# A fused attention and expert kernel on one core: packs, rows of maxima, score banks and the order of projections around its first two attentions

## Reference

```python
x = x + L0_xattn(_layernorm(x), ctx)     # self-attention, cross-attention, FFN (1024), a norm behind each
x = x + L0_ffn(_layernorm(x))            # one 256x256 linear layer plus a low-rank part
x = x + L1_xattn(_layernorm(x), ctx)     # masked cross-attention, 77 keys
x = x + L1_ffn(_layernorm(x))            # gated single-head attention and 8 experts
```

```python
sa = _mha(x, x, x, Wq1, Wk1, Wv1, bv1, causal=True)      # 16 heads of 16, 1024 x 1024 scores
x  = layernorm(sa + x, g1, be1)
ca = _mha(x, ctx, ctx, Wq2, Wk2, Wv2, bv2, causal=False) # 77 keys
x  = layernorm(x + ca, g2, be2)
x  = layernorm(x + relu(x @ Wf1 + bf1) @ Wf2 + bf2, g3, be3)
```

## Time and profile before

| | us |
|---|---|
| median of 3 runs (1371.41 to 1375.86) | 1371.98 |
| the profiled execution | 1369.3 |
| its span in the trace | 1367.3 |

### The profile page before, as it was taken

The page is one execution under the profiler, slowest core; times in us unless marked ns, Lnnn a source line. Parts: engine busy times, 40 slices in busy tenths (PEclk is TensorE's granted clock), DMA queues, the critical chain, the costliest instruction groups (busy, mean ns, idle before and its releaser), DMA issues. The chain is left out here.

```text
span 1367.3 us, 19836 instructions
## 1 busy us (share of the span) xinstructions
PE 1201.6 (88%) x7072; PEld 844.6 (62%) x7072; DVE 856.5 (63%) x1816; ACT 565.2 (41%) x1202; POOL 315.6 (23%) x490
## 2 busy tenths in 40 slices
PE   7888888888888798999888786899989888899999
PEld 3443333323333336677667665899977777688998
DVE  4487666677656666666568786766644355955555
ACT  5215566656565553455225542210013233543332
POOL 5011222222121036444127651000010111500000
PEclk8999999999998767999889987999999989999999
DMA  5850373330444601000011000000030000000000
GB/s 198 166 131 1 55 62 47 48 48 1 70 72 71 122 4 56 1 1 1 1 74 50 2 0 1 1 1 1 0 123 1 0 1 1 1 1 17 16 17 16
DMA packets 37968, 50.69 MB, mean 37 GB/s; under 512 B 11098, under 2 KB 28784, under 8 KB 37232
## 3 DMA queue, kind: packets, MB, share of 16 engines
q1 hardware_dynamic: 37872, 49.44, 17.3%
HBM read 37.26 MB, written 11.77 MB: 36 GB/s over the span
## 5 line engine op out<-in xcount | busy, mean ns | idle before, releaser
L545 PE MATMUL PS<-ARENA 128*17 128x512 f32 (+17 forms) x2208 | 410.1, 430 | 71.2 <-DVE ARENA L1708 23.9
L545 PEld LDWEIGHTS PS<-ARENA 128*17 128x17 f32 (+6 forms) x2208 | 164.5, 127 | 249.7 <-issue 109.9
L1322 ACT ACTIVATE ARENA<-PS 128x512 f32<-128x512 f32 (+3 forms) x384 | 177.0, 491 | 140.8 <-PE PS L545 134.6
L1708 DVE TENSOR_REDUCE ARENA<-PS 128x1 f32<-128x128 f32 (+7 forms) x256 | 179.7, 750 | 74.1 <-PE PS L545 73.3
L545 PE MATMUL PS<-WQKVP,TRR 128*128 128x384 f32 x512 | 133.0, 341 | 3.1 <-DVE ARENA L2012 2.0
L2174 POOL TENSOR_SCALAR_AFFINE_SELECT ARENA<-ARENA 128x128 f32<-128x128 f32 x256 | 74.9, 299 | 202.5 <-ACT ARENA L1322 198.6
L2142 POOL TENSOR_TENSOR rstd<-var,halves 128x4 f32<-128x4 f32 x36 | 38.4, 1065 | 281.9 <-DVE var L1553 232.7
L545 PEld LDWEIGHTS PS<-W2P,INT 128*128 128x128 f32 x768 | 95.1, 188 | 2.9
L545 PE MATMUL PS<-W2P,INT 128*128 128x256 f32 x768 | 95.5, 280 | 0.0
L545 PEld LDWEIGHTS PS<-WQKVP,TRR 128*128 128x128 f32 x512 | 92.6, 190 | 4.1 <-DVE ARENA L2012 2.3
L545 PE MATMUL PS<-TRR,W1P 128*128 128x512 f32 x256 | 88.4, 406 | 7.1 <-ACT BC L1248 7.1
(11 more groups left out here) (228 smaller groups left out, 1971.9 us busy)
## 6 DMA issues: line engine op xcount, KB each, us to landing
ARENA<-qk_parts SPq DMA_DIRECT2D x96, 128.0 KB, 5.7
...
ARENA<-in_w SPq DMA_DIRECT2D x2, 2048.0 KB, 10.8
...
```

The costliest lines, as they stand in the source:

```text
L545: return nc.tensor.matmul(o, lhsT, rhs, start=start, stop=stop, **kw)
L1322: ins = nc.scalar.activation(PROB[GRP * (step % 2) + j][:, 0:w], PS[:, uses[key][0], 0:w], ACT.Exp, scale=HD ** -0.5)
L1708: ins = v.tensor_reduce(negm[:, n % 2, TPB * j + st:TPB * j + st + 1], PS[:, bank:bank + 2, :].rearrange("p b s -> p (b s)")[:, 0:P * (st ...
```

## The change

It has five parts.

- **Start.** The projections of a batch run chunk by chunk (`projection`), so that the first needs only its first chunk's transposes. SP stores the 64 rows of group 0 first and loads its query half and key half each as soon as that half's store has landed; `load_pack(1)` comes after all stores of batch 0. Fillers before the first maximum: 8 for 36.
- **Third score bank.** Self-attention's scores use banks 4, 5 and 7; both halves of the values share bank 6, and every group's output is copied and turned in two halves (`evach`, `outh`), the first in the middle of its own block.
- **Chunk order.** The second chunk's queries are made in block 7 instead of 8, and SP stores them before group 7's rows of maxima. In block 8 the maxima of chunks 0 and 1 come one per unit, and norm, turn and queries of chunk 2 some units earlier.
- **Third chunk's packs.** `XPACK[2]` lies in ranges of its own (part of `SA` and `VEXT` that batch 0 used), so SP loads it without waiting for the last scores; `XPROB` moves and the cross stage's output goes to `XO`. Rows of chunks 2 and 3 are issued by POOL, behind `xneg` in its order. Some slots move up by one to three, and `xpv` of eight steps (`FILLED_STEPS`) gets 2 fillers.
- **Last norm.** Pieces 1 to 5 of the fourth chunk's second norm come after DVE's split of the FFN's second weight, and POOL's power for it after its first eight lower parts.

```diff
             if u == 1 and n > 1:
-                yield "evac", n - 2
+                yield "evach", n - 2, 1
             if u == OUT_AT and n > 1:
-                yield "out", n - 2
+                yield "outh", n - 2, 1
+            if u == 19 and n > 0:
+                yield "evach", n - 1, 0
+            if u == 23 and n > 0:
+                yield "outh", n - 1, 0
...
                 yield from context_plan(u - 6)
-            if n in (7, 8):
-                c, at = n - 7, u - (8, 2)[n - 7]
-                if at in (0, 2):
-                    yield "xq", c, at // 2
-                if at in (4, 6):
-                    yield "xqm", c, at // 2 - 2
+            if n == GROUPS - 1:
+                for c, first in enumerate((8, 26)):
+                    at = u - first
+                    if at in (0, 2):
+                        yield "xq", c, at // 2
+                    if at in (4, 6):
+                        yield "xqm", c, at // 2 - 2
             if n == GROUPS:
-                if u == 20:
-                    yield "evach", n - 1, 0
+                if u < 8:
+                    yield "xmax", 0, u % 4, u // 4
+                if u == 9:
+                    yield "xneg", 0
+                if 14 <= u < 22:
+                    yield "xmax", 1, (u - 14) % 4, (u - 14) // 4
                 if u == 23:
-                    yield "outh", n - 1, 0
-                if u >= 25 and u % 2 == 1 and u < 25 + 2 * NORM_PIECES:
-                    yield "norm", 2, u // 2 - 12
-                if u == 43:
+                    yield "xneg", 1
+                if 24 <= u < 24 + NORM_PIECES:
+                    yield "norm", 2, u - 24
+                if u == 37:
                     yield "turn", 2
-                if u in (45, 47):
-                    yield "xq", 2, u // 2 - 22
-            if n == GROUPS and u % 2 == 0:
-                if 6 <= u < 22:
-                    yield "xmax", 0, (u - 6) // 2 % 4, (u - 6) // 8
-                if u == 22:
-                    yield "xneg", 0
-                if u >= 32:
-                    yield "xmax", 1, (u - 32) // 2 % 4, (u - 32) // 8
+                if u in (39, 41):
+                    yield "xq", 2, u // 2 - 19
+                if u in (44, 46):
+                    yield "xqm", 2, u // 2 - 22
...
     yield "evach", GROUPS - 1, 1
-    yield "xneg", 1
...
+def projection(step):
+    g, at = divmod(step, 4)
+    return g, at % 2, at // 2
...
     yield from out(XSTEPS - 1)
+FILLED_STEPS = (0, 5, 6, 7, 11, 12, 13, 14)
...
     put(0, 0, "outh", GROUPS - 1, 1)
-    for g in range(2):
-        put(0, 1 + g, "xqm", 2, g)
     for piece in range(NORM_PIECES):
-        put((piece + 3) // 4, (piece + 3) % 4, "norm", 3, piece)
-    put(3, 0, "turn", 3)
-    put(3, 2, "xq", 3, 0)
+        put((piece + 1) // 4, (piece + 1) % 4, "norm", 3, piece)
+    put(2, 3, "turn", 3)
+    put(3, 1, "xq", 3, 0)
...
     put(4, 2, "xqm", 3, 1)
-    for m, (t, j) in enumerate(((3, 1), (3, 2), (4, 0), (4, 3), (5, 0), (5, 1), (5, 2), (5, 3))):
+    for m, (t, j) in enumerate(((2, 1), (3, 0), (3, 2), (4, 0), (4, 3), (5, 0), (5, 1), (5, 2))):
         put(t, j, "xmax", 2, m % 4, m // 4)
-    put(6, 0, "xneg", 2)
-    for piece, (t, j) in enumerate(((6, 2), (6, 3), (7, 0), (7, 1), (7, 2))):
+    put(5, 3, "xneg", 2)
+    for piece, (t, j) in enumerate(((6, 0), (6, 1), (6, 2), (6, 3), (7, 0))):
...
         XPACK = [[region(lo, 2048).bitcast(BF16).rearrange("p (h s) -> p h s", h=HH) for lo in pair]
-                 for pair in ((4096, 10240), (0, 6144), (2048, 8192), (4096, 10240))]
+                 for pair in ((4096, 10240), (0, 6144), (14336, 22528), (4096, 10240))]
...
         KPARTS = region(30736, 462).bitcast(BF16).rearrange("p (g c t) -> p g c t", g=2, c=3)
-        XPROB = [region(22528 + 512 * s, 512, parts=T) for s in range(8)]
+        XPROB = [region(lo + 512 * j, 512, parts=T) for lo in (8192, 24704) for j in range(GRP)]
+        XO = region(2048, 2048, "p (i f) -> p i f", i=2 * GRP)
...
             return c if rest == 0 and 0 <= c < 4 else None
+        def load_rows(eng, c):
+            eng.wait_ge(xmparts_ready, c + 1)
+            for g in range(2):
+                for r in range(3):
+                    eng.dma_start(XPACK[c][g][ROWS + r:ROWS + r + 1, :, :].rearrange("o h (t s) -> o (h t) s", s=P),
+                                 xmparts[32 * g:32 * g + 32, c % 2, r, :]).then_inc(xrows_in[c], 16)
...
                 banks = ((2, 3, 4, 5, 6, 7), (6, 7, 4, 5))[b]
-                if step == 0:
-                    for c in (2 * b, 2 * b + 1):
-                        turn("t_in", "in", H, c, ((0, 1), (4, 5))[b], 14 if c == 0 else 0)
-                    for c in (2 * b, 2 * b + 1):
-                        turned("t_in", c)
+                if step < 2:
+                    turn("t_in", "in", H, 2 * b + step, ((0, 1), (4, 5))[b], 14 if (b, step) == (0, 0) else 0)
+                if step in (0, 2):
+                    turned("t_in", 2 * b + step // 2)
                 if step < 8:
-                    g, w, c = step // 4, step // 2 % 2, step % 2
+                    g, w, c = projection(step)
...
                             claim("idle", [0], 0, 0)
-                            busy(36, 0)
+                            busy(8, 0)
...
                     w = 512 * c + 512 - lo
-                    bank = 4 + narrow
+                    bank = (4, 5, 7)[ring % 3]
...
                     filled(ins, ("score", n, tt, c, j))
-                    narrow = 1 - narrow
+                    ring += 1
...
                     if (tt, c) == (0, 0):
-                        if n < GROUPS - 1:
-                            claim(("values", n), [6, 7], signals=0)
-                        else:
-                            for half in range(2):
-                                claim(("values", n, half), [6 + half], signals=0)
+                        claim(("values", n, 0), [6], signals=0)
...
                             drained(pe, ("v1", i))
+                    if (tt, c) == (0, 1):
+                        claim(("values", n, 1), [6], signals=0)
...
                     for j in range(GRP):
-                        ins = mm(PS[32 * j:32 * j + VW, 6 + c, lo - 512 * c:512],
+                        ins = mm(PS[32 * j:32 * j + VW, 6, lo - 512 * c:512],
...
                     claim(("xv", n), [bank])
+                    busy(2 if n in FILLED_STEPS else 0, bank)
...
                      a[name].rearrange("(o e) -> o e", o=1).broadcast_to([P, EXPERTS]))
+            def load_half_pack(n, w):
+                b, h0 = n // 4, GRP * (n % 4)
+                packs, order = ((PACKQ, QPART), (PACKK, KPART))[w]
+                src = scratch[b, w].rearrange("(h e) c s -> c e h s", h=HEADS)
+                for r, part in enumerate(order):
+                    sp.dma_start(packs[n % SLOTS][HD * r:HD * r + HD, :, :],
+                                 src[part, :, h0:h0 + GRP, :]).then_inc(pack_in[n % SLOTS], 16)
             def load_pack(n):
-                b, h0 = n // 4, GRP * (n % 4)
-                for w, packs, order in ((0, PACKQ, QPART), (1, PACKK, KPART)):
-                    src = scratch[b, w].rearrange("(h e) c s -> c e h s", h=HEADS)
-                    for r, part in enumerate(order):
-                        sp.dma_start(packs[n % SLOTS][HD * r:HD * r + HD, :, :],
-                                     src[part, :, h0:h0 + GRP, :]).then_inc(pack_in[n % SLOTS], 16)
-            for u in range(8):
-                b, g, w = u // 4, u // 2 % 2, u % 2
-                sp.wait_ge(parts_ready, 2 * (u + 1))
-                sp.dma_start(scratch[b, w, P * g:P * g + P, :, :], PARTS[u % 4]).then_inc(parts_out[u], 16)
-                if u == 1:
-                    for v in (0, 1):
-                        sp.wait_ge(parts_out[v], 16)
-                    load_pack(0)
-                    load_pack(1)
+                for w in range(2):
+                    load_half_pack(n, w)
+            def store_parts(b, g, w, lo=0, hi=P):
+                sp.wait_ge(parts_ready, 8 * b + 4 * g + w + 3)
+                sp.dma_start(scratch[b, w, P * g + lo:P * g + hi, :, :], PARTS[2 * g + w][lo:hi]).then_inc(parts_out[4 * b + 2 * g + w], 16)
+            for w in range(2):
+                store_parts(0, 0, w, 0, GRP * HD)
+            for w in range(2):
+                sp.wait_ge(parts_out[w], 16)
+                load_half_pack(0, w)
+            for w in range(2):
+                store_parts(0, 0, w, GRP * HD, P)
+            for w in range(2):
+                store_parts(0, 1, w)
+            for w in range(2):
+                sp.wait_ge(parts_out[w], 32)
+            load_pack(1)
+            for u in range(4):
+                store_parts(1, u // 2, u % 2)
...
                     load_pack(n + 2)
-            send_queries(1)
...
             load_queries(1)
-            load_rows(0)
-            load_rows(1)
+            load_rows(sp, 0)
+            load_rows(sp, 1)
```

(37 more changed lines are left out.)

92 lines of the change are left out of this document (37 added, 55 removed).

## The result

The changed kernel takes 1355.07 us (median of 4 runs, 1352.71 to 1356.99) against 1371.70 (4 runs, 1371.14 to 1375.86) of the kernel before: a ratio of 0.9872, 95% interval 0.9846 to 0.9897. Timed again beside other kernels it was 1352.49 against 1367.66, 0.989 (0.9848 to 0.9932). So the change gains 15 to 17 us, about half of the 32.8 of the forecast. 1355 lies inside the range given (1323 to 1361), but not in the 1328 to 1350 to which the forecast gave 0.45.

A forecast was written before the change was run, and what follows sets the result against it. TensorE's (PE's) order of work, its waits and its clock were taken to bound the kernel; 7 + 1 + 6 + 2 + 14 + 2.8 = 32.8 us gained, giving 1339 us (forecast 1328 to 1350, range 1323 to 1361).

The forecast's parts named there:

- block 8: Self-attention's block 8: score waits go and chunk 0's row maxima come one per score; 2 us gained, bounds -2 and 4.
- (a): Cross stage keeps its low clock because light work, not waits, lowers it; no gain there, total 1353 us; chance 0.20.
- (c): Cross stage: POOL issues DMAs at 2 us each, each chunk's rows come 6.6 us later; total 1352 us; chance 0.10.
- Start: Before the first maximum: chunk-first projections and half packs bring it from 51 to 44 us; 7 gained, bounds 4 and 9.
- (e): Start: half packs fail because stores keep the DMA engines full; gain 0 to 2 us, total 1345 us; chance 0.08.
- Block 0: Self-attention's first block, 51 to 101 us: PE idles less though its clock still falls; 1 us gained, bounds -1 and 3.
- Third score bank: Blocks 1 to 7: scores stop waiting for exponentials in block tails, up to 0.89 us each; 6 us gained, bounds 0 and 10.
- the mark set for a wrong prediction: Self-attention: the prediction counts as wrong if blocks 1 to 7 together are not 3 us shorter.
- Cross stage: Cross stage: earlier packs, rows from POOL's queue and fillers cut 93.5 us to 79.5; 14 gained, bounds -7 and 24.
- (d): Cross stage: POOL's DMA issues dearer still, eating the whole gain at 3.6 us each; over 1376 us from 4.0; chance 0.04.
- the clock term: Cross stage: two thirds of PE's 56 us at the lower clock level are lifted, within the 14 us gain.
- FFN: Start of the FFN: PE's 3.34 us wait for DVE's split of the second weight falls under 0.5; 2.8 gained, bounds 0 and 3.

The follow-up runs named there:

- the two bank runs: Changed kernel with two score banks instead of three: ratio 0.9869 to the kernel before; the same with the values' halves in banks of their own: 0.9890.

## Why the forecast held only by half

The stages in three readings, in us gained: the forecast; the two profiled executions (12.0 between their spans); and the means over all profiles in which a stage ran the same code as before (2 or 3) or as after (5 to 9). The points are SP's issue of block 0's rows, its issue of block 6's, PE's first cross score, the fillers ahead of the FFN, and the second products.

| part | forecast | one pair | means |
|---|---|---|---|
| start and block 0 | 7 + 1 | 8.5 - 2.5 | 6.9 - 3.3 = 3.6 (95.7 to 92.1) |
| blocks 1 to 6 | 6, with block 7 | -1.0 | -0.5 (233.3 to 233.9) |
| blocks 7 and 8 | 2 (block 8) | -0.5 | -1.6 (90.4 to 92.1) |
| cross stage | 14 | 1.2 | 4.8 (95.2 to 90.4) |
| start of the FFN | 2.8 | 5.1 | 5.4 (21.7 to 16.3) |
| behind it | 0 | 1.3 | about 4, what the runs' means leave |

The 4.8 of the cross stage lean on one profile: the stage of before took 93.0, 93.1 and 99.5 us, and without the last the gain is 2.7.

That 1355 us fell into the range is due to its width. It lies next to the 1353 and 1352 of rivals (a) and (c), and neither of them is what happened; the terms that failed were partly made up by some 4 us that no step had forecast and by a start of the FFN that gave twice its term.

**Start, right.** 42.5 lies half a microsecond below the 43 to 44.5, and over all profiles the first maximum came at 42.3 to 44.6 (mean of the nine with 8 fillers 43.2, of before 50.0): 6.9 gained of the 7 forecast. Rival (e) did not come about. The estimate that PE would be ready at 41 was off: it was ready at 36. So the load is last by 6 us and not by 3, and that was the cover for more fillers.

**Block 0, wrong in sign.** The step said that the clock would still fall, and gave it no price. It costs 5.3 us with 8 fillers in the pair of profiles with 8 and 36, and 4.3 over all of them. Where the forecast took 1 us of gain, the block became 3.3 longer on average.

**Third score bank, the second wrong step.** Its price came out, 0.85 against 0.89, in good part by luck: the sum took it from the tail's waits for ACT, and the tail gave 0.34 and kept such waits (three of 0.36 us); the rest came from narrow scores elsewhere in the block. "Copy and output are split in two ... nothing" was wrong: 0.55 a block, shown by the two bank runs. That ACT and DVE are idle for 41% and 32% of the stage said nothing about the moment at which the halves come. Blocks 1 to 7 were not 3 us shorter, which was the mark set for a wrong prediction. Why blocks 7 and 8 together became 1.6 us longer was not tried apart; chunk 1's projection and PE's wait of 2.09 us for chunk 2's norm lie there, and two profiles with a clock of 0.93 in block 7 (94.5 and 94.7 us, the others 91.0 to 91.6) make half of it.

**Cross stage, the step that failed most.** The forecast let chunk 2's wait fall from 3.57 to about 1 "since from POOL's queue they start as soon as DVE is done". They did start then, but chunk 2's wait came out at 5.14 (3.2 to 5.1 over five profiles) and chunk 3's at 3.09: the prediction's own reading, that the rows had run among 1.5 MB of chunk 3's pack, went on holding. That pack was again issued just ahead of them, and the rows come when it is through. Rivals (c) and (d) did not come about, POOL's issues being cheap (0.52 us). With the waits as long as before, the clock term failed too: I counted on two thirds of 56 us of low time being lifted, and (1 - 0.80) x 2 x 92.3 = 37 of them stayed, so a third was. The 16 fillers of the steps, which were to do it, show no effect. That fillers inside the waits do bring the gain is shown by 82.7 and 80.7 us, about the 79.5 of the forecast. The earlier trace rows came again, a clock of 0.50 at 5.00 us busy of 5.00, 6 us behind the 3.09 us wait; with that wait filled the 22.2 us behind it ran at 1.00 (19.5 us busy). So it is the wait and not the work that takes the clock down. Whether this light work is slow to bring it back up stays open. Rival (a), that the light work lowers the clock, is refuted by 0.99 and 1.00 from near step 12 on with the same work.

**FFN, right, too small.** The wait fell to 0.73, not quite under the 0.5 that was to show it. The term was taken at the clock of one execution; at the higher level the same wait is 6.5 us.

**Behind the FFN** no step of the change acts. About 4 us at the end go with the clock, 0.935 against 0.930 over the whole run; this is argued from the 0.31 us above and not shown apart. The profiles agree in size, 828.4 us from the second products to the end for before (three) and 823.8 for the change and its variants (eleven), but the same code there takes 814.5 to 831.6 from one execution to the next, so it may also be chance.
